# The last two feed-forward chunks written out behind a step loop, tables and split halves made during an earlier attention

## The reference, cut to what matters

```
for i in range(DEPTH):                       # 6
    x = attn_layer(shift_tokens(x), Wqkv[i], q_scale[i], k_scale[i], Wo[i]) + x
    x = ffn_layer(shift_tokens(x), ln_g[i], ln_b[i], W1[i], b1[i], W2[i], b2[i]) + x
ffn: xn = layernorm(x) * g + b; a, gate = split(xn @ W1 + b1)
     return a * gelu(gate) @ W2 + b2
```

## Time and profile before

| | |
|---|---|
| median of 3 runs | 1726.53 us (1721.86, 1726.53, 1729.63) |
| the profiled execution | 1727.49 us |
| its span in the profile | 1725.7 us |
| mean granted clock of TensorE | 0.987 of full |
| TensorE busy | 1598.7 us (93%) |
| VectorE, ScalarE, GpSimd busy | 1357.6, 1279.7, 1292.0 us |

### The profile page before, as it was taken

One profiled execution on the slowest core, in us unless ns is written; L12 is line 12 of the kernel. 1 busy time (PEld: TensorE's weight loads), 2 busy tenths in 40 slices (PEclk: granted clock), 3 DMA queues, 4 the chain that ended last, 5 costly groups with the idle time before them and its releaser, 6 DMA issues.

```text
span 1725.7 us, 70625 instructions
## 1 busy us (share of the span) xinstructions
PE 1598.7 (93%) x29308; PEld 1222.0 (71%) x29308; DVE 1357.6 (79%) x1876; ACT 1279.7 (74%) x1888; POOL 1292.0 (75%) x1227
## 2 busy tenths in 40 slices
PE   8999988899899999999998999998999998999996
PEld 5778866666677767677776777776777776777774
DVE  5677867787788887888888888887888887888873
ACT  3788846777677787677778867776887787788673
POOL 3222159888888888888898878889888988888871
PEclk8999999999999999999999999999999999999998
DMA  5111213533324333334333334333343333333331
GB/s 166 49 45 41 54 26 74 131 85 92 87 67 107 102 84 94 82 82 129 81 90 91 81 89 117 83 93 96 71 127 83 89 88 79 85 76 76 82 78 45
DMA packets 127629, 146.51 MB, mean 85 GB/s; under 512 B 58448, under 2 KB 71504, under 8 KB 125776
## 3 DMA queue, kind: packets, MB, share of 16 engines
q1 hardware_dynamic: 127312, 141.98, 33.4%
HBM read 25.47 MB, written 1.05 MB: 15 GB/s over the span
## 4 chain that ended last, share of the span: by engine, by line
PE 64%; ACT 10%; issue 8%; DVE 7%; POOL 5%; SPq 4%; DMA 1%; DVEq 0%; POOLq 0%; ACTq 0%
PE banks L1261 39%; PE banks L1562 7%; PE banks L1517 7%; PE banks L1622 6%; PE banks L1407 4%; SPq L414 2%; ACT vst L839 2%; ACT banks L854 2%; DVE arena L1103 2%; POOL prob L576 1%; ACT arena L796 1%; DVE small L1132 1%; SPq L376 1%; POOL arena L586 1%; DVE small L1138 1%
## 5 line engine op out<-in xcount | busy, mean ns | idle before, releaser
L581 POOL TENSOR_TENSOR arena<-arena 128x1024 f32<-128x1024 f32 x96 | 230.2, 2397 | 67.2 <-DVE arena L1103 67.0
L1150 DVE TENSOR_REDUCE small<-banks 128x16 f32<-128x1024 f32 x96 | 117.6, 1225 | 199.8 <-PE banks L1562 199.7
L839 ACT ACTIVATE vst<-banks 128x1024 f32<-128x1024 f32 x192 | 196.7, 1024 | 79.8 <-PE banks L1261 67.8
L1098 DVE TENSOR_TENSOR arena<-banks,tabs 128x1024 f32<-128x1024 f32 x192 | 233.7, 1217 | 19.1 <-ACT arena L796 17.5
L1103 DVE TENSOR_TENSOR arena<-banks,tabs 128x1024 f32<-128x1024 f32 x192 | 233.3, 1215 | 0.0
L586 POOL TENSOR_TENSOR arena<-arena 128x1024 f32<-128x1024 f32 x96 | 228.7, 2382 | 0.0
L576 POOL TENSOR_TENSOR prob<-prob,small 128x1024 f32<-128x1024 f32 x96 | 184.3, 1919 | 25.7 <-DVE small L1140 25.6
L1261 PE MATMUL banks<-qkH,xsH 128*128 128x512 f32 x384 | 177.2, 461 | 24.7 <-DVE arena L1103 12.7
L1562 PEld LDWEIGHTS banks<-arena 64*32 64x32 f32 x12288 | 134.7, 106 | 90.2 <-issue 87.5
L1562 PE MATMUL banks<-arena 64*32 64x64 f32 x12288 | 166.5, 225 | 33.6 <-ACT banks L854 23.3
L1622 PE MATMUL banks<-arena 128*32 128x128 f32 x6144 | 190.7, 277 | 1.0 <-issue 1.0
(11 more groups left out here) (149 smaller groups left out, 3760.3 us busy)
## 6 DMA issues: line engine op xcount, KB each, us to landing
arena<-vst SPq DMA_DIRECT2D x1536, 64.0 KB, 2.0
qkraw<-in_wqk_dram SPq DMA_DIRECT2D x6, 1024.0 KB, 6.0
arena<-in_wvo_dram SPq DMA_DIRECT2D x5, 1024.0 KB
tabs<-in_tab_dram SPq DMA_DIRECT2D x40, 128.0 KB, 2.6
gq<-w1w SPq DMA_DIRECT2D x64, 64.0 KB, 2.0
lns<-Xt SPq DMA_DIRECT2D x96, 32.0 KB
lns<-Xt SPq DMA_DIRECT2D x96, 31.8 KB
xsH<-w1w SPq DMA_DIRECT2D x32, 64.0 KB, 2.0
```

The costliest lines, as they stand in the source:

```text
L581: pool.tensor_tensor(kc, kc, ks, ALU.add).then_inc(s["k_add"], 1)
L839: act.activation(vst[:, g, :], two(V_BANK), ACT.Copy).then_inc(s[f"v_cp{g}"], 1)
L1098: dve.tensor_tensor(heads(c), heads(two(0)), table(k % NT, kind), ALU.mult).then_inc(s[done], 1)
```

## The change

The loop of each engine ends earlier: TensorE and VectorE run steps 0 to 97, ScalarE 0 to 96, GpSimd 0 to 100. Behind it the rest is written out. The last two chunks become three spans: span 0 is chunk 22 (tiles 88 to 91, 512 columns), span 1 tiles 92 to 94 (384 columns), span 2 tile 95 (128 columns). Each has gates, gelus, values, products, down product and residual of its own, on PSUM banks named in tables, and the output goes out in five writes in place of four.

GpSimd scales the tables of tiles 0 to 3 at its beginning and those of tiles 4 to 7 behind the splits of the long attention, and there makes the halves of all four column chunks. For this the query copies gQ now lie in MH (and its lower half ML, as before) and no longer in xsH and xsL. `first_steps` is gone. The idle products of before stay, and two sets of seven stand in the written-out end.

```diff
-STEPS = DEPTH * TILES + 11
+STEPS = DEPTH * TILES + 5
+LOOPED = DEPTH * NC - 2
+SPANS = ((DEPTH * NC - 2, 0, CH), (DEPTH * NC - 1, 0, 3 * P), (DEPTH * NC - 1, 3 * P, CH))
+SPAN_GATES = ((0, 1, 7), (1, 2, 3), (1, 2, 3))
+SPAN_VALUES = ((4, 5, 0), (4, 5, 0), (4, 5, 0))
+SPAN_DOWN = (7, 7, 6)
-        gQ = [xsH[:, 1, 0:T], xsL[:, 1, 0:T], gq2[:, 0, :], gq2[:, 1, :]]
+        gQ = [a.rearrange("p q m n -> p (q m n)")[:, T * z:T * (z + 1)] for a in (MH, ML) for z in range(2)]
@@ chunk_at
-            return c if (G - lag) % 4 == 0 and 0 <= c < DEPTH * NC else None
+            return c if (G - lag) % 4 == 0 and 0 <= c < LOOPED else None
@@ SyncE
-                sp.dma_start(out_t[:, 4 * c:4 * c + 4, :], res[:, 4 * c:4 * c + 4, :]).then_inc(out_in, 16)
+                tiles = slice(4 * c, 4 * c + 4 if c < NC - 1 else TILES - 1)
+                sp.dma_start(out_t[:, tiles, :], res[:, tiles, :]).then_inc(out_in, 16)
+            sp.wait_ge(s["fin_add"], NC + 1)
+            sp.dma_start(out_t[:, TILES - 1, :], res[:, TILES - 1, :]).then_inc(out_in, 16)
@@ GpSimd
-            for n in range(2):
+            for n in range(NT // 2):
                 scale_table(0, n, n + 1)
...
-            for c in range(2):
+            for c in range(NC):
                 upper_first(c)
                 lower_shifted(c)
+            for n in range(NT // 2, NT):
+                scale_table(0, n, n + 1)
...
-            def first_steps(k):
-                if k < NT - 2:
-                    scale_table(0, k + 2, k + 3)
-                if k in (2, 3):
-                    pool.wait_ge(s["gL_mm"], NSTEP)
-                    pool.wait_ge(s["gS_mm"], NSTEP)
-                    upper_first(k)
-                    lower_shifted(k)
@@ ScalarE
+            def span_gelus(n):
+                c, c0, c1 = SPANS[n]
+                for j in range(3):
+                    m = FJ[j][1]
+                    if n < 2:
+                        act.wait_ge(s["f_mm"], LOOPED + n)
+                    act.wait_ge(s[f"g_mm{j}"], LOOPED + 1 + n)
+                    act.activation(gl[j][0:m, c0:c1], bk(SPAN_GATES[n][j])[0:m, 0:c1 - c0], ACT.Gelu, bias=b1p[0:m, 3 + j:4 + j])\
+                       .then_inc(s[f"gl{j}"], 1)
-            for G in range(STEPS):
+            for G in range(LAST_TILE + 2):
...
+            normalise_rows(LAST_TILE - 3)
+            exponentials(LAST_TILE)
+            copy_columns(LAST_TILE - 3)
+            roots(LAST_TILE + 2)
+            copy_probs(LAST_TILE)
+            act.preload_act_table_set("gelu_and_others")
+            span_gelus(0)
+            act.preload_act_table_set("natural_log_exp_and_others")
+            normalise_rows(LAST_TILE - 2)
+            copy_columns(LAST_TILE - 2)
+            roots(LAST_TILE + 3)
+            normalise_rows(LAST_TILE - 1)
+            copy_columns(LAST_TILE - 1)
+            roots(LAST_TILE + 4)
+            normalise_rows(LAST_TILE)
+            span_gelus(1)
+            copy_columns(LAST_TILE)
+            span_gelus(2)
@@ VectorE, behind the loop of steps 0 to 97
+            denominators(LAST_TILE)
+            moments(LAST_TILE - 2)
+            lower_columns(LAST_TILE - 3)
+            moments(LAST_TILE - 1)
+            attended(LAST_TILE)
+            for j in range(3):
+                span_gated(0, j)
+            lower_columns(LAST_TILE - 2)
+            lower_columns(LAST_TILE - 1)
+            moments(LAST_TILE)
+            span_residual(0)
+            for j in range(3):
+                span_gated(1, j)
+            lower_columns(LAST_TILE)
+            span_residual(1)
+            for j in range(3):
+                span_gated(2, j)
+            span_residual(2)
@@ TensorE, behind the loop of steps 0 to 97
+            ln_columns(LAST_TILE - 3)
+            for j in range(3):
+                span_gate(0, j)
+            span_value(0, 0)
+            span_value(0, 1)
+            transpose_probs(LAST_TILE)
+            weigh(LAST_TILE)
+            span_value(0, 2)
+            idle_products(3, 7)
+            ln_columns(LAST_TILE - 2)
+            idle_products(3, 7)
+            ln_columns(LAST_TILE - 1)
+            span_down(0)
+            for j in range(3):
+                span_gate(1, j)
+            for j in range(3):
+                span_value(1, j)
+            ln_columns(LAST_TILE)
+            span_down(1)
+            for j in range(3):
+                span_gate(2, j)
+            for j in range(3):
+                span_value(2, j)
+            span_down(2)
```

More of the change, by code:

```diff
@@ L449, in _ @@
                 sp.wait_ge(s["fin_add"], c + 1)
-                sp.dma_start(out_t[:, 4 * c:4 * c + 4, :], res[:, 4 * c:4 * c + 4, :]).then_inc(out_in, 16)
-            sp.wait_ge(out_in, 16 * NC)
+                tiles = slice(4 * c, 4 * c + 4 if c < NC - 1 else TILES - 1)
+                sp.dma_start(out_t[:, tiles, :], res[:, tiles, :]).then_inc(out_in, 16)
+            sp.wait_ge(s["fin_add"], NC + 1)
+            sp.dma_start(out_t[:, TILES - 1, :], res[:, TILES - 1, :]).then_inc(out_in, 16)
+            sp.wait_ge(out_in, 16 * (NC + 1))
         @block.gpsimd
@@ L666, in _ @@
                 clear_values(G)
-                first_steps(G)
                 next_key_weights(G)
@@ L1230, in _, with span_gated, span_residual @@
             folded_lower(0, 1)
-            for G in range(STEPS):
+            def span_gated(n, j):
+                c, c0, c1 = SPANS[n]
+                m = FJ[j][1]
+                dve.wait_ge(s[f"a_mm{j}"], LOOPED + 1 + n)
+                dve.wait_ge(s[f"gl{j}"], LOOPED + 1 + n)
+                dve.scalar_tensor_tensor(gl[j][0:m, c0:c1], bk(SPAN_VALUES[n][j])[0:m, 0:c1 - c0], b1p[0:m, j:j + 1], gl[j][0:m, c0:c1],
+                                         ALU.add, ALU.mult).then_inc(s[f"h{j}"], 1)
+            def span_residual(n):
+                c, c0, c1 = SPANS[n]
+                t0, t1 = c % NC * 4 + c0 // P, c % NC * 4 + c1 // P
+                dve.wait_ge(s["f_mm"], LOOPED + 1 + n)
+                dve.tensor_tensor(Xt[:, t0:t1, :], bk(SPAN_DOWN[n])[:, 0:c1 - c0].rearrange("p (t d) -> p t d", d=D), Xt[:, t0:t1, :], ALU.add)\
+                   .then_inc(s["x_new"], 1)
+                dve.wait_ge(s["x_new"], LOOPED + 1 + n)
+                dve.tensor_tensor(res[:, t0:t1, :], Xt[:, t0:t1, :], res[:, t0:t1, :], ALU.add).then_inc(s["fin_add"], 1)
+            for G in range(LAST_TILE + 3):
                 sum_keys(G - 1)
@@ L1696, in layer_columns, with span_up, span_gate, span_value @@
                     freed[XT_BANK] = ("xs", 2 * (c + NC) + 2)
-            for G in range(STEPS):
+            def span_up(n, at, j):
+                c, c0, c1 = SPANS[n]
+                f, (j0, m) = c % 2, FJ[j]
+                i = (SPAN_GATES if at else SPAN_VALUES)[n][j]
+                w = slice(at + j0, at + j0 + m)
+                pe.wait_ge(s["xn_L"], 4 * c + c1 // P)
+                claim(i)
+                mm(bk(i)[0:m, 0:c1 - c0], W1H[:, w], xnH[f][:, c0:c1], True, False)
+                mm(bk(i)[0:m, 0:c1 - c0], W1L[:, w], xnH[f][:, c0:c1], False, False)
+                return mm(bk(i)[0:m, 0:c1 - c0], W1H[:, w], xnL[f][:, c0:c1], False, True)
+            def span_gate(n, j):
+                span_up(n, FF, j).then_inc(s[f"g_mm{j}"], 1)
+                freed[SPAN_GATES[n][j]] = (f"gl{j}", LOOPED + 1 + n)
+            def span_value(n, j):
+                span_up(n, 0, j).then_inc(s[f"a_mm{j}"], 1)
+                freed[SPAN_VALUES[n][j]] = (f"h{j}", LOOPED + 1 + n)
+            def span_down(n):
+                c, c0, c1 = SPANS[n]
+                for j in range(3):
+                    pe.wait_ge(s[f"h{j}"], LOOPED + 1 + n)
+                o = bk(SPAN_DOWN[n])
+                claim(SPAN_DOWN[n])
+                for t in range(c0 // P, c1 // P):
+                    for j in range(3):
+                        m = FJ[j][1] + (j == 2)
+                        ins = mm(o[:, P * t - c0:P * (t + 1) - c0], gl[j][0:m, P * t:P * (t + 1)], W2[0:m, (DEPTH - 1) % 2, j, :], j == 0, j == 2)
+                ins.then_inc(s["f_mm"], 1)
+                freed[SPAN_DOWN[n]] = ("x_new", LOOPED + 1 + n)
+            for G in range(LAST_TILE + 3):
                 project_queries_last(G - 1)
```

## The result

The changed kernel takes 1710.68 us in the median of five runs (1705.31 to 1712.46), the kernel before 1721.87 us in five runs next to it (1721.44 to 1729.63). The ratio is 0.9921, with a 95% interval of 0.9902 to 0.994: faster by 10.3 to 16.9 us; the two medians lie 11.2 us apart. Forecast were 1717.4 us, 1712 to 1722.5, and 9.1 us of gain. In all that follows, one execution of a variant (without the idle products) that took 2141.42 us at a mean granted clock of 0.635 is left out of the ratios.

The account below looks back on a forecast made before the run. TensorE was taken to hold most of the chain, except in the first steps and the end. Gains of 1.8 + 8.0 - 0.7 = 9.1 us from the median 1726.53 gave 1717.4 us, range 1712 to 1722.5.

Parts of the forecast that it names:

- The rise of the front, 1.8 us: First loop steps: moving GpSimd's tables and halves out gains 1.8 us, bounds 0.7 and 5.6.
- That 7.5 us of moved work cost nothing: Behind the long attention's splits: the moved tables and halves, 7.5 us, fit into GpSimd's 34.5 us of idleness.
- ScalarE as the pace, 14.1 us to the normalised tile 95: End: ScalarE sets the pace; tile 95 normalised 14.1 us behind the roots' end, before 15.9.
- 8.65 us from there to the last add: End: from tile 95's normalising to the last add 8.65 us in place of 14.86, gaining 6.2 us.
- The end's clock, minus 0.7 us: End: a 3 us stretch at half clock on TensorE, 0.7 us subtracted, bounds 0 and 3.9.
- The write, 2.73 us kept: Last output write: 64 KB in place of 256, still counted at 2.73 us, up to 0.4 less.
- the sum's term for the end, 8.0 minus 0.7: Whole end: tail gain 8.0 us at full clock, less 0.7 us for half clock.
- (b): First steps: waits gone, clock stays up, loop starts 4 to 5 us earlier; short write; gain 10.8 to 14.5; chance 0.18.
- (a): End gains little: half clock persists, idle products push columns, small matmuls cost more; gain 3 to 7.5; chance 0.18.
- (c): Slower: granted clock at half over the whole end, 1731.5 us against the median; chance 0.03.
- (d): End: table loads drain as in the page's rule, shifting ScalarE's chain 2.8 us; 1720.2 us; chance 0.02.
- (e): First steps give nothing, as another chain (mask, vst) is the bound; 1719.2 us; chance 0.09.

Follow-up runs that it names:

- end only: The changed kernel with the front of before, so only the end written out, against the kernel before: ratio 0.9953, 8.1 us.
- the second profile of the changed kernel: The changed kernel run again without edit, against the kernel before: ratio 0.993, 12.1 us.
- in the third: The changed kernel run once more without edit, against the kernel before: ratio 0.9944, 9.7 us.
- front only: The kernel before with only the tables and halves moved and gQ in MH, against the kernel before: ratio 0.9986, 2.4 us.

## Why the prediction came out as it did

Its steps, one by one:

- **The rise of the front, 1.8 us:** 2.4 by the times, with an interval from nothing to 4.8, and 2.2 to 2.6 at the twelfth mask. The first step's 0.65 is right (0.7, in every profile). For steps 2 and 3 I had counted 1.05 us more, as the mask bounds them; at the third mask the first profile has 1.3 more, and 2.1 more lie between two executions without a stretch at half clock (end only and the second profile of the changed kernel). So the bound was somewhat too tight; by how much at the end of the steps, the scatter hides.
- **That 7.5 us of moved work cost nothing:** right, 21.3 us of idleness are left.
- **ScalarE as the pace, 14.1 us to the normalised tile 95:** 14.17. This sum is right by luck in one part: the three gelus took 1.83 us in place of 2.07, and a wait I had missed took it back. I let the rows of tile 95 go out as soon as it was attended; they are held 2.5 us on SyncE for tile 93. The stall I had named, the moments queued behind tile 94's columns, exists, and this wait lies beneath it.
- **8.65 us from there to the last add:** 8.71. The matmuls of 128 columns go at some 0.11 us each.
- **The end's clock, minus 0.7 us:** nothing in the first profile, 1.6 us in the second, nothing in the third and in end only. As a mean of four that is 0.4.
- **The write, 2.73 us kept:** 2.0. I had allowed for up to 0.4 less; it was 0.7, in each of the four profiles.

What failed is the sum's term for the end, 8.0 minus 0.7, that is 7.3, where 8.6 are measured in the trace (8.1 by the times of the end alone). Piece by piece: 1.7 to the normalised tile 95 (forecast 1.8), 6.15 from there to the last add (6.2), 0.7 of the write (forecast none), and no loss by the clock (forecast 0.7). So the chain of waits was right, and its two side terms, the clock and the write, make the difference. With the front's 2.6 us that makes 11.2 in place of 9.1. That 11.2 us is also the distance of the two medians is partly luck: the later comparisons gave 12.1 and 9.7 us for the same kernel.

The larger part of the miss is the base. The time lies 6.7 us under the forecast: 2.1 of them are gain, 4.7 the base. 1726.53 us was the median of three runs, and four comparisons with 5 to 18 runs of before (the first counts these three among its five) put it at 1721.87, 1723.68, 1722.34 and 1724.07; so 2.5 to 4.7 us of that base were scatter. The profile from which I took the rows could have warned me: its execution starts with 13.7 us at half clock, where nine of the eleven others read here have 3.4 us between 27 and 37 us. The forecast and its range were hung on that base.

The chance of faster, 0.18 + 0.35, adds up to 0.53 and not to 0.54; nothing hangs on it. Of the signs of being wrong none came, but one was near: the moments of tile 95 start 9.74 us behind the roots' end, and 10 was the mark.

Of the rivals, (b) has the size: 11.2 us lie in its 10.8 to 14.5, and the short write that it named came. Its main mechanism isn't borne out. Between the clear and the twelfth mask the changed kernel's three profiles have two, one and three stretches at half clock of 3.4 us, and before has three; in steps 2 and 3 the first and third of them have such a stretch and the second has none, and end only, which keeps all the waits of before, has none there either: its first begins 57.6 us behind the clear, behind the third mask. So the clock there doesn't follow these waits. (a), (c) and (d) didn't come; (e) is refuted by the first and third masks, though not by the times of front only, whose interval touches it.

Open stays what else scatters a program's executions, by 7 to 10 us for the changed kernel and by 12 us for before: from the first mask to the roots' end the three profiles of the changed kernel took 1438.8, 1436.4 and 1443.8 us, with three, one and three stretches of 3.4 us at half clock. The first and the third have the same number and lie 5.0 us apart.

## What to carry to other kernels

When a tail is written out, follow each buffer's reuse on the DMA queue too: here an attended tile waited 2.5 us for a read that ScalarE had put behind a gelu, and the trace shows it only as a late issue. Where one wait lies beneath another, expect less than the sum from removing the upper one, and look at the granted clock of the execution before you call a move worthless: one stretch at half clock cost as much (1.0 us) as the move was to give. And where runs scatter by 0.5%, price a change from marks inside several traces, and don't anchor the forecast on the median of three runs.

## What the runs showed of the hardware

The same code in the same order meets different clocks: near 26 us the granted clock falls for 3.4 us in one execution of the changed kernel and for 13.7 in another, and the clear of kT comes at 219.49 and at 223.38 us. Behind the same wait of 2.04 us, 18 down passes took 2.25 us in one execution and 3.47 in another. With two sets of seven idle products of 512 columns behind the weighing, the 24 down passes that follow took 2.92 us in eight profiles of eight; in the one profile without them 5.40. Beside a table load the gelu starts 1.30 us behind the load's start, in both kernels. Three gelus of 512 columns in a row take 1.83 us, 0.61 each, where single ones show 0.69.
